# All rows of a group gathered by GpSimd, none by one-hot products on TensorE, in a four-layer graph network

## The reference

```python
x = (og_x @ W).reshape(N, N_HEADS, HEAD_DIM)
alpha_l = jnp.sum(x * att_l, axis=-1)
alpha_r = jnp.sum(x * att_r, axis=-1)
alpha = alpha_l[src] + alpha_r[dst]
...
seg_max = jax.ops.segment_max(alpha, dst, num_segments=N)
...
exp_a = jnp.exp(alpha - seg_max[dst])
seg_sum = jax.ops.segment_sum(exp_a, dst, num_segments=N)
coef = exp_a / (seg_sum[dst] + 1e-16)
msg = x[src] * coef[:, :, None]
agg = jax.ops.segment_sum(msg, dst, num_segments=N)
```

## Time and profile before

| | us |
|---|---|
| median of 3 runs | 4386.61 (4384.65 to 4387.99) |
| span of the profiled execution | 5825.1 |
| busy: PE, DVE, ACT, POOL | 3173.4, 3165.7, 2409.4, 2312.0 |
| gathers, L1400 | 2184, 949 ns each |

### The profile page before, as it was taken

How to read it: one execution, slowest core, us unless ns; L and a number is a source line. 1 busy time by engine, 2 the same in 40 slices (tenths; PEclk the granted TensorE clock), 3 DMA queues, 4 the chain that set the end, 5 groups by cost and what they waited for, 6 DMA issues and landing times. The chain is left out here.

```text
span 5825.1 us, 61632 instructions
## 1 busy us (share of the span) xinstructions
PE 3173.4 (54%) x16208; PEld 1958.6 (34%) x16208; DVE 3165.7 (54%) x10115; ACT 2409.4 (41%) x5229; POOL 2312.0 (40%) x2409
## 2 busy tenths in 40 slices
PE   2888787623555555562155554555523555564563
PEld 1333343312333333342033333333311333343342
DVE  5999853513454554576064464555822455454466
ACT  0766630023444444443143443444433444444453
POOL 3000002074555455415545545544064545545422
PEclk7999998856777677786577777777756777777786
DMA  2111124221212222111112212211021212212110
GB/s 75 60 60 60 60 85 168 99 62 36 48 46 48 47 47 50 42 28 37 42 45 48 52 44 48 50 46 44 4 55 37 47 47 47 50 45 47 45 25 23
DMA packets 127624, 298.46 MB, mean 51 GB/s; under 512 B 45412, under 2 KB 74972, under 8 KB 123712
## 3 DMA queue, kind: packets, MB, share of 16 engines
q0 software_dynamic: 74976, 155.58, 11.6%
q1 hardware_dynamic: 52320, 139.24, 7.1%
HBM read 241.28 MB, written 53.38 MB: 51 GB/s over the span
## 5 line engine op out<-in xcount | busy, mean ns | idle before, releaser
L1400 POOL DMA_INDIRECT work<-table,lane_src x2184 | 2072.7, 949 | 1897.4 <-PE psum L1554 967.3
L1439 ACT ACTIVATE work<-work,middle_node_number 128x384 f16<-128x384 f16 x1587 | 958.0, 604 | 1997.8 <-DMA work<-table,lane_src 950.8
L1497 PE MATMUL psum<-work 128*128 128x396 bf16 (+1 forms) x5850 | 1360.1, 380 | 699.7 <-issue 464.9
L1554 PE MATMUL psum<-work 128*128 128x136 f32 x4836 | 827.7, 339 | 1004.9 <-DVE node_sums L1722 890.6
L1722 DVE TENSOR_TENSOR node_sums<-node_sums,psum 128x136 f32 x2418 | 561.3, 294 | 1455.8 <-remote 892.2
L1554 PEld LDWEIGHTS psum<-work 128*128 128x128 f32 x4836 | 778.8, 242 | 1085.0 <-issue 969.9
L1497 PEld LDWEIGHTS psum<-work 128*128 128x128 bf16 x5850 | 626.3, 109 | 1290.0 <-issue 758.1
L1442 ACT ACTIVATE work<-work 128x384 bf16<-128x384 f16 x1587 | 829.4, 523 | 50.4
L715 PE MATMUL psum<-work 128*128 128x448 f16 x2100 | 460.9, 358 | 47.4 <-issue 37.5
L744 DVE TENSOR_SCALAR work<-work 128x400 f16<-128x400 f16 x1568 | 468.3, 320 | 0.0
L772 PE MATMUL psum<-work 128*128 128x400 f16 x1568 | 342.1, 342 | 111.8 <-DVE work L744 90.9
(11 more groups left out here) (360 smaller groups left out, 2539.9 us busy)
## 6 DMA issues: line engine op xcount, KB each, us to landing
counts<-work SPq DMA_DIRECT2D x14, 2800.0 KB, 8.1
work<-counts SPq DMA_DIRECT2D x14, 2800.0 KB
work<-table,lane_src POOLq DMA_INDIRECT x2184
work<-spread SPq DMA_DIRECT2D x78, 256.0 KB
work<-masks SPq DMA_DIRECT2D x78, 128.0 KB
work<-source_rows SPq DMA_DIRECT2D x39, 192.0 KB
spread<-node_sums SPq DMA_DIRECT2D x4, 896.0 KB
table<-work SPq DMA_DIRECT2D x10, 330.0 KB
```

What stands on the lines that cost most here:

```text
L1400: pool.indirect_dma_start(m.ring[:, s % SLOTS, 0:F + H], None, m.d_table[H], bass.IndirectOffsetOnAxis(ap=m.src[:, s:s + 1], axis=0)).then ...
L1439: act.activation(away, rows_of(g, u), ACT.Abs, bias=m.low_tile[:, hi:hi + 1]).then_inc(far_known, 1)
L1497: mm = pe.matmul(aid_banks[:, k, 0:3 * (F + H)], hot_of(g, u)[:, k * P:(k + 1) * P], m.all_thirds[:, :, hi, 0:F + H], start=(hi == 0), sto ...
L1554: pe.matmul(sum_slot(s), m.onehot[b % 2][:, s % U, :], m.ring[:, s % SLOTS, :], start=True, stop=True).then_inc(product, 1)
```

## The change

All 64 steps of a group are fetched by GpSimd. What goes: the units on TensorE, the one-hots on ScalarE and VectorE, `take_aided`, the three bf16 parts and the operations that make them in the node stage, the source rows in DRAM, their store and their broadcasts on SyncE. The three banks of PSUM that the units had become a second set for the products: `sum_slot` alternates by block, and the products of a block wait for the sums of two blocks before. The ring, the groups and the chain stay. In the node stage TensorE's next product waits for the table copies and not for the low part.

```diff
-    def gathered(b):
-        return [s for s in steps_of(b) if place(s) >= AIDED]
...
     def sum_slot(s):
-        at = (2 + s % U // PER_BANK) * 512 + s % U % PER_BANK * W
+        at = (2 + s // U % 2 * BLOCK_BANKS + s % U // PER_BANK) * 512 + s % U % PER_BANK * W
...
-                for s in gathered(b):
+                for s in steps_of(b):
                     pool.indirect_dma_start(m.ring[:, s % SLOTS, 0:F + H], None, m.d_table[H],
...
-                if g >= 2:
-                    sp.wait_ge(hot_used, (g - 1) * UNITS)
-                sp.dma_start(m.aid_rows[g % 2], m.d_src_rows[own.start:own.start + AIDED, :].rearrange("(a s) e -> a (s e)", a=1)
...
                     for s in steps_of(b):
-                        if s % U % PER_BANK == 0 and s >= U:
-                            pe.wait_ge(summed, bank_end(s - U))
+                        if s % U % PER_BANK == 0 and s >= 2 * U:
+                            pe.wait_ge(summed, bank_end(s - 2 * U))
...
-                    for n in parts_of(g, b):
-                        aid(g + 1, part_of[n])
...
-                        for u in itertools.chain(*(part_of[k] for k in parts_of(g, b))):
-                            if u in by_dve:
-                                hot_on_dve(dve, g + 1, u)
...
-                    if g + 1 < GROUPS and n in TAKEN_IN:
-                        take_aided(g + 1, TAKEN_IN.index(n))
...
-                    pe.wait_ge(thirds_known, len(parts) * (b - 1))
+                    pe.wait_ge(tables, per_block * (b - 1))
...
-                for n, (lo, hi) in enumerate(parts):
-                    act.copy(high[:, c * BLK + lo:c * BLK + hi, :], out_part(c, n)[:, :, 0:F + H]).then_inc(high_taken, 1)
-                if c:
-                    middles(c - 1)
```

More of the change, by code:

```diff
@@ L221, in allocate @@
     at += 4 * P
[L222 to L233, removed]
     assert at <= ARENA
@@ L1692, in onehot @@
                                   over(m.drel[:, b * U:b * U + n].unsqueeze(2), [P, n, P]), ALU.is_equal).then_inc(hot, 1)
-            def take_aided(g, n):
-                third = [aid_banks[:, :, i * (F + H):(i + 1) * (F + H)] for i in range(3)]
-                lo = lo_of(g) + n * PER_BANK
-                rows = slots(lo, PER_BANK)[:, :, 0:F + H]
-                dve.wait_ge(hot_used, g * UNITS + (n + 1) * NODE_TILES)
-                if lo >= SLOTS:
-                    dve.wait_ge(product, lo + PER_BANK - SLOTS)
-                chain(dve.tensor_copy(rows, third[2]))
-                chain(dve.tensor_tensor(rows, rows, third[1], ALU.add))
-                dve.tensor_tensor(rows, rows, third[0], ALU.add).then_inc(aid_taken, 1)
-                dve.wait_ge(aid_taken, g * PASSES + n + 1)
             def places_of(lo, n):
@@ L1726, in _ @@
             dve.wait_ge(cleared, 2)
-            for u in range(UNITS):
-                if u % 2:
-                    hot_on_dve(dve, 0, u)
-                if u % NODE_TILES == NODE_TILES - 1:
-                    take_aided(0, u // NODE_TILES)
             spread(0)
@@ L1893, in scores @@
                 dve.engine_nop().then_inc(spread_known, 1)
-            def rest(b):
-                dve.wait_ge(high_taken, len(parts) * (b + 1))
-                for n, (lo, hi) in enumerate(parts):
-                    j = slice(b * BLK + lo, b * BLK + hi)
-                    product = out_part(b, n)[:, :, 0:F + H]
-                    dve.tensor_tensor(product, product, high[:, j, :], ALU.subtract).then_inc(rest_known, 1)
-            def lowest(b):
-                dve.wait_ge(middle_taken, len(parts) * (b + 1))
-                for n, (lo, hi) in enumerate(parts):
-                    j = slice(b * BLK + lo, b * BLK + hi)
-                    dve.tensor_tensor(low[:, j, :], out_part(b, n)[:, :, 0:F + H], middle[:, j, :], ALU.subtract).then_inc(thirds_known, 1)
-            for wave in range(TURNS + last + 3):
+            for wave in range(TURNS + last + 2):
                 for i, step in enumerate(steps):
@@ L1954, in _ @@
         def _(act):
-            def middles(b):
-                act.wait_ge(rest_known, len(parts) * (b + 1))
-                for n, (lo, hi) in enumerate(parts):
-                    j = slice(b * BLK + lo, b * BLK + hi)
-                    act.copy(middle[:, j, :], out_part(b, n)[:, :, 0:F + H]).then_inc(middle_taken, 1)
             for wave in range(TURNS + last + 1):
```

142 lines of the change are left out of this document (14 added, 128 removed).

## The result

The changed kernel takes 4651.07 us (median of 4 runs, 4648.05 to 4654.76), the kernel before 4385.63 us (4 runs, 4383.68 to 4387.99): a ratio of 1.0607, 95% interval 1.0592 to 1.0622. It is 265 us slower. The forecast was 4670 us, +283. The profiled execution of the changed kernel has its own time of 4649.47 us and a span of 4647.0 us: unlike the one of before, it runs as the other runs do.

What follows compares the result with a forecast made beforehand. GpSimd's gathers were taken as the bound: 4386.61 us + 293.4 for 234 more gathers - 10 for the node stages, all else 0, gives 4670 us, 6.5% slower; forecast 4635 to 4706, wider range 4565 to 4715.

Steps and rivals of the forecast that it cites:

- Gathers bind, 1.25 us start to start: GpSimd's gathers in the attention layers: they bound the kernel, each costing 1.254 us start to start.
- All of it on the path: GpSimd's gathers: 234 more at 1.254 us add 293.4 us, all to the kernel's time if GpSimd binds.
- VectorE's 8.9 us a group worth nothing in the steady groups: VectorE's chain: one-hots, takes and a wait go, 8.9 us a group, hidden under the gathers: 0.
- Node stages: ScalarE's casts ahead of the scatters: fewer pairs, three layers together -10 us, between 0 and -16.
- TensorE's clock and the second set of banks at 0: TensorE's slower clock and products waiting only for sums two blocks before: 0 each; clock at most 35.6 us in tails.
- My reading is that these stalls belong to the recorded execution: Attention layers: 138 VectorE waits, 1334.8 us, occur only in the profiled execution, not in the runs.
- Nothing stops it from running without a pause: GpSimd's gathers: they wait only for ring slots freed a group ago, so GpSimd should bind the runs.
- The test: Whole kernel before, stalls removed: 1501.7 outside attention, 120.7 tails, 2738.7 gathers, sum 4361.1 against 4386.61 us measured.
- one sign in the prediction: Profile of the changed kernel: its recorded span would again hold stalls, more of them (151).
- 1: Attention groups: gathers not the bound, 0.949 us each, VectorE's chain sets the end; 4030 us, faster; chance 0.09.
- 2: Attention groups: gathers at about 1.11 us near VectorE's chain, little change, 4380 us; chance 0.03.
- 3: Gathers bound but held up by VectorE's one-hots (L1387); removal returns 101 us, 4569 us; chance 0.06.
- 4: GpSimd's stops behind each 16 gathers are real: 44 us more, 4714 us, slower still; chance 0.06.

Runs made afterwards that it cites:

- e7_bbank: Kernel before, with TensorE updating the product semaphore once a bank (24 a group in place of 64): 4384.37 us, 1.0001 of the kernel before.
- e8_two: Changed kernel with 16 more two-input VectorE operations a group behind the cap of the scores: 4704.43 us, 1.0731 of the kernel before.
- e1_aid3: Kernel before with one TensorE pass of three steps a group instead of two, 61 gathers a group: 5680.68 us, 0.9766 of the kernel before.
- e10_after: Changed kernel, unaltered, on a chip of the second kind: 5660.82 us against 5894.09 us for the kernel before, 0.9593.
- e10_block: Changed kernel with one TensorE semaphore update for each block's products (8 a group, not 64): 5556.40 us against 5894.09 us for the kernel before, 0.9425.

## Why the prediction was right, and where not

The parts of the time, worked out from the source views by layer of e7_bbank (standing for the kernel before) and of the changed kernel; first and last start, us, of the gathers and of the sums, for the three layers of e7_bbank:

```profile
L1403 POOL DMA_INDIRECT work<-table,lane_src x728: 947/952/1188, 1161.9 to 2081.9; - x182
...
L1727 DVE TENSOR_TENSOR node_sums<-node_sums,psum x806: 275/295/299, 1254.4 to 2131.2; 128x136 f32 x162
...
L1403 POOL DMA_INDIRECT work<-table,lane_src x728: 940/944/1426, 2236.6 to 3163.0; - x182
...
L1727 DVE TENSOR_TENSOR node_sums<-node_sums,psum x806: 275/295/298, 2330.3 to 3218.3; 128x136 f32 x162
...
L1403 POOL DMA_INDIRECT work<-table,lane_src x728: 940/944/1178, 3309.5 to 4223.0; - x182
...
L1727 DVE TENSOR_TENSOR node_sums<-node_sums,psum x806: 275/295/298, 3401.2 to 4271.9; 128x136 f32 x162
```

and of the changed kernel:

```profile
L1317 POOL DMA_INDIRECT work<-table,lane_src x806: 947/952/1189, 1159.7 to 2179.3; - x162
...
L1574 DVE TENSOR_TENSOR node_sums<-node_sums,psum x806: 282/295/298, 1257.3 to 2220.5; 128x136 f32 x162
...
L1317 POOL DMA_INDIRECT work<-table,lane_src x806: 940/945/1441, 2324.1 to 3351.9; - x162
...
L1574 DVE TENSOR_TENSOR node_sums<-node_sums,psum x806: 281/295/299, 2425.3 to 3396.3; 128x136 f32 x162
...
L1317 POOL DMA_INDIRECT work<-table,lane_src x806: 940/945/1182, 3484.1 to 4498.2; - x162
...
L1574 DVE TENSOR_TENSOR node_sums<-node_sums,psum x806: 281/295/298, 3581.5 to 4538.6; 128x136 f32 x162
```

With 0.3 us for the last sum, in us:

| | e7_bbank | changed | difference | predicted |
|---|---|---|---|---|
| first to last gather, three layers | 920.0 + 926.4 + 913.5 = 2759.9 | 1019.6 + 1027.8 + 1014.1 = 3061.5 | +301.6 | +293.4 |
| last gather to last sum | 49.6 + 55.6 + 49.2 = 154.4 | 41.5 + 44.7 + 40.7 = 126.9 | -27.5 | 0 |
| ahead of and between the layers | 1161.9 + 105.1 + 90.9 = 1357.9 | 1159.7 + 103.3 + 87.5 = 1350.5 | -7.4 | -10 |
| behind the last sum | 109.6 | 108.1 | -1.5 | 0 |
| span | 4381.8 | 4647.0 | +265.2 | +283.4 |

**Gathers bind, 1.25 us start to start: right.** The pace is 1.266 to 1.268 us, not 1.254. Nearly all of the 12 ns are gathers beside VectorE's score stage. Of the 2184 gathers of e7_bbank 183 are over 40 ns longer than 944, together 31 us; in the recording of before, where GpSimd often pauses in that stage, only 70 are, together 7 us. The difference is 11 ns a gather. In the changed kernel 203 of 2418 are, 40 us. Most of that is beside operations of VectorE with two inputs in SBUF, element by element or scans. The earlier trace rows has no such gather; the changed kernel's timeline, GpSimd and VectorE in the score of the second layer, has:

```profile
3061.79 0.69 DVE L1472 TENSOR_TENSOR work<-psum,work 128x512 f32<-128x512 f32 x1 [24.31 <-PE psum L1385]
3062.51 0.69 DVE L1475 TENSOR_TENSOR work<-work 128x512 f32<-128x512 f32 x1
3062.70 1.32 POOL L1317 DMA_INDIRECT work<-table,lane_src  x1 [0.31 <-issue]
...
3068.38 0.94 POOL L1317 DMA_INDIRECT work<-table,lane_src  x1 [0.30 <-issue]
...
3069.56 0.69 DVE L1505 TENSOR_TENSOR work<-work 128x512 f32<-128x512 f32 x1
...
3069.63 1.44 POOL L1317 DMA_INDIRECT work<-table,lane_src  x1 [0.30 <-issue]
```

The Trainium skill, page "SBUF — State Buffer", section "Who interferes with whom", names this case too, an operation of VectorE with two SBUF inputs beside a GpSimd instruction that reads SBUF, where I had weighed only its other one, the two-port modes. The trace agrees that the two get in each other's way: 1.32 us beside L1475 and the two operations behind it, 1.44 us beside L1505 and what follows it, and 1.15 us in e8_two, against 0.94. The same section of the Trainium skill also tells of a probe in which `tensor_tensor` did not stall DMAs; here it lengthens their issue, and the measurement decides. That the ports are the reason is not shown by these runs.

**"All of it on the path", for the 293.4 us of gathers: the term that failed.** The tails, from a layer's last gather to its last sum, fell by 27.5 us, and the prediction had nothing there. A layer's last group has 46 steps and the one before it 56. The kernel before fetches only 40 for the last, 40 x 1.266 = 50.6 us, while VectorE's chain of the group ahead takes 59.4 us. The starts and waits of the last three scores in e7_bbank:

```profile
4113.63 0.42 DVE L1613 TENSOR_TENSOR work<-psum,work 128x256 f32<-128x256 f32 x1 [10.14 <-PE psum L1517]
4176.52 0.42 DVE L1613 TENSOR_TENSOR work<-psum,work 128x256 f32<-128x256 f32 x1 [1.30 <-PE psum L1517]
4235.89 0.41 DVE L1613 TENSOR_TENSOR work<-psum,work 128x256 f32<-128x256 f32 x1
```

and in the changed kernel:

```profile
4372.96 0.42 DVE L1472 TENSOR_TENSOR work<-psum,work 128x256 f32<-128x256 f32 x1 [26.36 <-PE psum L1385]
4443.65 0.42 DVE L1472 TENSOR_TENSOR work<-psum,work 128x256 f32<-128x256 f32 x1 [16.15 <-PE psum L1385]
4502.49 0.42 DVE L1472 TENSOR_TENSOR work<-psum,work 128x256 f32<-128x256 f32 x1 [8.91 <-PE psum L1385]
```

The last score of the kernel before waits for nothing: VectorE was late by itself. In the changed kernel it waits 8.91 us, gather-bound to the end. The last gather and the last group's column copy, in e7_bbank and then in the changed kernel, show the same:

```profile
4223.01 0.94 POOL L1403 DMA_INDIRECT work<-table,lane_src  x1 [0.30 <-issue]
...
4233.66 0.83 ACT L1461 COPY work<-work 128x32 f32<-128x32 f32 x6 [6.05 <-DVE work L1708]
```

```profile
4498.21 0.94 POOL L1317 DMA_INDIRECT work<-table,lane_src  x1 [0.30 <-issue]
4501.42 0.23 ACT L1353 COPY work<-work 128x24 f32<-128x24 f32 x1 [7.86 <-DMA work<-table,lane_src]
```

Before, the copy comes 10.7 us behind the last gather and waits for VectorE's take of TensorE's rows (L1708, `take_aided`); after, it comes 3.2 us behind and waits for the gather. The prediction's own rows had this: in the earlier trace rows the last column copies wait for L1703, the same take, and yet it began the tail at this copy, as if the copy stood right behind the last gather.

So the last group's six more gathers, 7.6 us, ran in time for which VectorE had been the bound (its last score starts 12.9 us behind the last gather in e7_bbank, 4.3 us in the changed kernel): 18 of the 234 cost nothing (18 x 1.268 = 22.8 us). With the rest, (234 - 18) x 1.268 - 7.4 - 1.5 = 265.0 us, measured 265. That it fits to under 1 us is partly luck: two terms of some 5 us that it leaves out cancel. The tails fell by 4.7 us more than 22.8, since VectorE's chain is shorter without the take and the one-hots, and all gathers together are 5 us slower by pace, 1.268 for 1.266.

**VectorE's 8.9 us a group worth nothing in the steady groups: right.** VectorE's wait grew from 11.2 us a group in e7_bbank to 1058.0 / 39 = 27.1. The chain is 57.6 us in the eight-head layer, within the 54 to 59 foreseen. **Node stages:** -7.4 us against -10; about right. From their first scatter the 25 scatters of a node stage end 2.4, 1.8 and 3.3 us sooner than in e7_bbank, where 3 was foreseen. **TensorE's clock and the second set of banks at 0:** borne out by the sum on a chip of the first kind, though never tested there alone. The mean granted clock in the attention layers is 0.84 in e7_bbank and 0.63 in the changed kernel, and the tails got shorter all the same. On chips of the second kind the second set seems to save some 3%: 0.9878 without it, 0.9593 with it, each against the kernel before on its own chip; no two runs on one chip show it.

**"My reading is that these stalls belong to the recorded execution": wrong.** Step by step the evidence was there: 138 stalls of 10 us, both engines resuming within 0.13 us of each other. "Nothing stops it from running without a pause" was against the earlier trace rows, which put 967.3 us of GpSimd's idle time down to L1554, the products that free its ring slots. What the step lacked was the third possibility, that profile and times came from chips that behave differently. On which chips they were taken is not on record, but plain runs at 5817 us on one and at 4384 us on another leave little else. The stalls are real where they occur; they did not occur where 4386.61 us was measured. The forecast survived because it took its pace from between the stalls and tested the sum against the median of the runs. The test was passed by luck in part: 1501.7 us outside the layers is 1467.5 us in e7_bbank (34 too much; the first gather starts at 1161.9, and at 1194 to 1200 on every chip of the second kind), and the tails are 154.4 and not 120.7 (34 too little). Both errors cancel to under 1 us, and the 25.5 us left over are the pace (12 ns x 2184 = 26 us). For the same reason one sign in the prediction failed: the recorded span of the changed kernel, 4647.0 us, holds no stalls. And its chances for the range add up to 0.88, where it says 0.86.

**Rivals.** 1 and 2 needed a pace under 1.11 us; it is 1.266. 3 is out, with no sign of GpSimd held up by L1387: the pace did not fall when it went. 4, stalls real in the runs, was taken for 4714 us at a chance of 0.06. Its premise holds on chips of the second kind, but its sign is the opposite there: a pass taken off TensorE saves time on such a chip (e1_aid3), and by the comparison above the second set of banks does too, together more than the gathers cost. A prediction for a chip that behaves as the profile does would have had to be 4% faster (e10_after, 5661 us against 5894).

## What to carry to other kernels

When a profile's span and the times of the runs differ by far more than the runs among themselves (here by a third), they may come from chips that behave differently; the sum must be made for both, and the sign of a change can differ between them. Where a queue of one engine is the bound, its start-to-start pace times the count gave the time within 0.6% here, before and after. The ends of a phase need a look of their own: in the last, shorter group another engine may be the bound, and added work is free; the row of its first operation says what it waited for. An engine's idle time absorbs added work only as far as that work leaves the bounding engine alone.

## What the runs showed of the hardware

- One and the same program takes 4384 us on one chip and 5817 to 5894 us on four others, each within 0.5% over its runs. On the slower ones many updates that TensorE makes of a semaphore while GpSimd's indirect DMAs run arrive late, up to 23.6 us in the stretch shown; of those over 3 us late in e10_block, 88 of 144 came while GpSimd paused, most of them 4.0 to 4.4 us behind its last gather. VectorE's updates, as far as the trace has them, are on time (median 0.011 us).
- A gather of 128 rows has a pace of 1.25 us from start to start, and 1.45 us beside a run of operations of VectorE with two float32 inputs in SBUF (0.94 becomes 1.15 us, e8_two). Sixteen such operations a group inside VectorE's wait cost 55 us of 317, 27 us of them in the gathers.
